# A prologue in another order on one Trainium2 core: scans, first normalisations, activation tables

## The reference

```python
x = x + attn(bi_wkv(x, f, f, w1, u1, cond))
x = x + ffn(bi_wkv(x, f, f, w2, u2, cond))
```

```python
def bi_wkv(r, k, v, w, u, cond):          # forward and backward scans over time
    tf = sigmoid(sum(cond)); decay = exp(-exp(w)) * (0.5 + 0.5 * tf)
    ek = exp(min(k, 30)); ekv = ek * v
    nf, df, nb, db = scans with a = a * decay + ekv, b = b * decay + ek
    euk = exp(min(u + k, 30))
    num = nf + nb - ekv + euk * v; den = df + db - ek + euk
    return sigmoid(r) * num / max(den, 1e-8) * (0.8 + 0.2 * tf)

def attn(x):                              # time mix, then channel mix
    h = layernorm(x) ; hp = h shifted by one step in time
    r, k, v = sigmoid(mix(h, hp) @ Wr), mix(h, hp) @ Wk, mix(h, hp) @ Wv
    x = x + (r * exp(u + k) * v / (exp(u + k) + 1e-8)) @ Wout
    h2 = layernorm(x)
    return x + sigmoid(mix(h2) @ cWr) * (square(relu(mix(h2) @ cWk)) @ cWv)

def ffn(x):                               # 32 experts, 8 for each token, and a shared one
    shared = square(relu(x @ up)) @ down
    routed = (sum over 8 experts of weight * square(relu(x @ fc1 @ w1[e])) @ w2[e]) @ fc2
    return shared + routed
```

## Time and profile before

| | |
|---|---|
| timed, median of 3 | 1136.41 us (1134.61 to 1138.21) |
| profiled execution | 1126.11 us |
| its span | 1124.4 us |
| TensorE products busy | 1048.5 us, 93% |
| TensorE weight loads busy | 649.4 us, 58% |
| VectorE busy | 724.5 us, 64% |
| ScalarE busy | 513.0 us, 46% |
| GpSimd busy | 472.0 us, 42% |

### The profile page before, as it was taken

How to read it: one execution, slowest core, us unless ns; L and a number is a source line. 1 busy time by engine, 2 the same in 40 slices (tenths; PEclk the granted TensorE clock), 3 DMA queues, 4 the chain that set the end, 5 groups by cost and what they waited for, 6 DMA issues and landing times.

```text
span 1124.4 us, 13091 instructions
## 1 busy us (share of the span) xinstructions
PE 1048.5 (93%) x4094; PEld 649.4 (58%) x4095; DVE 724.5 (64%) x1346; ACT 513.0 (46%) x778; POOL 472.0 (42%) x432
## 2 busy tenths in 40 slices
PE   0479999999999999999999999998999999999788
PEld 0344444444444444554644444446999999999788
DVE  8998449999999999870787000003555555555376
ACT  4465525656565556341221111113666666666211
POOL 3533003532353236220008777662666666666500
PEclk9999999999999999999999999999999999999889
DMA  4563024432643211321204685357766776677398
GB/s 149 173 213 101 1 38 138 151 101 59 204 151 101 64 39 33 101 38 75 75 1 139 216 286 191 143 174 205 161 157 157 157 156 157 157 157 157 115 405 299
DMA packets 186322, 157.23 MB, mean 140 GB/s; under 512 B 113824, under 2 KB 159392, under 8 KB 184224
## 3 DMA queue, kind: packets, MB, share of 16 engines
q1 hardware_dynamic: 170336, 113.12, 35.6%
q0 software_dynamic: 15936, 43.53, 12.3%
HBM read 67.09 MB, written 68.55 MB: 121 GB/s over the span
## 4 chain that ended last, share of the span: by engine, by line
PE 75%; DVE 17%; issue 4%; DMA 2%; ACT 1%; POOL 0%; ACTq 0%; POOLq 0%; SPq 0%; DVEq 0%
PE banks L1596 24%; PE banks L605 13%; PE banks L616 12%; PE banks L570 10%; PE banks L543 10%; PE banks L675 2%; PE banks L519 2%; DMA arena<-parts 2%; DVE arena L1345 2%; PE banks L1611 2%; DVE arena L1336 2%; DVE arena L1334 1%; DVE arena L1447 1%; DVE arena L1438 1%; PE banks L665 1%
## 5 line engine op out<-in xcount | busy, mean ns | idle before, releaser
L1596 PE MATMUL banks<-arena 128*128 128x512 f32 x896 | 389.7, 595 | 12.2 <-DVE arena L1399 5.1
L1596 PEld LDWEIGHTS banks<-arena 128*128 128x128 f32 x896 | 170.3, 191 | 228.7 <-issue 216.9
L482 POOL DMA_INDIRECT parts<-arena x160 | 171.0, 1069 | 126.4 <-DVE arena L879 101.3
L474 POOL DMA_INDIRECT slots_in<-arena x128 | 129.2, 1010 | 91.1 <-issue 87.1
L605 PEld LDWEIGHTS banks<-arena 128*128 128x128 f32 x1280 | 156.8, 194 | 7.9 <-issue 3.9
L605 PE MATMUL banks<-arena 128*128 128x128 f32 x1280 | 157.4, 277 | 3.0 <-ACT arena L713 3.0
L616 PE MATMUL banks<-arena 128*128 x640 | 151.1, 379 | 0.0
L879 DVE TENSOR_TENSOR arena<-banks,arena 128x512 f32<-128x512 f32 x80 | 55.3, 691 | 119.9 <-PE banks L616 119.9
L616 PEld LDWEIGHTS banks<-arena 128*128 128x128 f32 x640 | 115.6, 190 | 12.5
L543 PE MATMUL banks<-arena 128*128 128x512 f32 x256 | 114.3, 592 | 0.0
L570 PE MATMUL banks<-arena 128*128 128x512 f32 x256 | 114.1, 592 | 0.0
(11 more groups left out here) (179 smaller groups left out, 1239.7 us busy)
## 6 DMA issues: line engine op xcount, KB each, us to landing
slots_in<-arena SPq DMA_DIRECT2D x20, 1120.0 KB, 5.9
arena<-parts SPq DMA_DIRECT2D x16, 1024.0 KB, 10.0
arena<-fT SPq DMA_DIRECT2D x32, 256.0 KB, 2.8
arena<-w2T SPq DMA_DIRECT2D x4, 2048.0 KB, 13.6
arena<-xT SPq DMA_DIRECT2D x4, 1024.0 KB, 7.9
arena<-xT POOLq DMA_DIRECT2D x4, 1024.0 KB, 9.7
arena<-w1T SPq DMA_DIRECT2D x2, 2048.0 KB, 13.1
out<-arena SPq DMA_DIRECT2D x16, 256.0 KB, 6.9
```

Source lines behind the costliest of these rows:

```text
L474: pool.indirect_dma_start(rows_in, bass.IndirectOffsetOnAxis(ap=POSU[:, n, j:j + 1], axis=0), XLR[:, n].bitcast(mybir.dt.uint32), None).th ...
L482: pool.indirect_dma_start(parts, bass.IndirectOffsetOnAxis(ap=DESTU[:, g:g + 1], axis=0), YO[:, i % 4, c], None).then_inc(y_sent[i % 4], 16)
L1596: ins = pe.matmul(out, w[:, k, m * P:(m + 1) * P], x[:, k], start=(k == 0), stop=(k == kt - 1))
```

## The change

Nothing is computed otherwise, but the condition's sigmoid, which becomes 1 / (1 + exp(-s)), with the exponential on ScalarE and the rest on VectorE. Everything else is order, and the grain of waits:

- Start: ScalarE loads the logarithm and exponential set at once. VectorE makes only the first mix column, clips the first keys, and then makes the decays; the forward scans of item 0 run ahead of the tables that need ScalarE's logarithm; four mix columns follow behind. `pre` is split in `pre_keys` and `pre_bonus`.
- After the first items: forward scans and one backward scan of batch 1's tile 0 come ahead of y tiles 0 to 2; fin, y tile 3, clip, the other backward scan; centring and squares of batch 0 and 1 by tiles (`center_tiles`, `square_tiles`), the variance's products waiting for each; bonus; normalise, mixes. The slots of tiles 1, 2 and 3 follow the mixes.
- TensorE: rkv of batch 0 runs through, then batch 1's mean, and batch 1's variance lies inside the output product. Batch 1's first mix is handed over by tiles. On VectorE two residuals and the forward and first backward scan of iteration 1's first item stand ahead of batch 1's normalisation.
- Experts: the first `own_w1` no longer waits for the shared expert's last product; VectorE copies the first rows ahead of the last sum; TensorE's first `m1` waits for one sum less.

The core of the diff (declarations of semaphores and small waits are left out):

```diff
-            pe.wait_ge(S['down_evac'], K * B)
+            pe.wait_ge(S['down_evac'], K * B - 1)
             pe.wait_ge(S['w1_loaded'], 16 * 8)
             pe.wait_ge(S['w2_loaded'], 64)
             m1(0, 0, 0)
+            pe.wait_ge(S['down_evac'], K * B)
...
+            own_w1(0)
             act.wait_ge(S['down_mm'], K * B)
-            own_w1(0)
...
-            down(dve, 3)
+            for m in range(K - 1):
+                down_tile(dve, 3, m)
...
+            dve.wait_ge(S['down_mm'], K * B)
             xT(0)
+            down_tile(dve, B - 1, K - 1)
...
+            act.preload_act_table_set("natural_log_exp_and_others")
...
-            act.activation(tf, bank(7)[:, 0:B], ACT.Sigmoid).then_inc(S['cond_ready'], 1)
+            act.activation(tf, bank(7)[:, 0:B], ACT.Exp, scale=-1.0).then_inc(S['cond_ready'], 1)
...
+            def square_tiles(b):
+                dst = squares(1, b)
+                for k in range(K):
+                    act.wait_ge(*((S['z_tile'], (K - 1) * b + k + 1) if k < K - 1 else (S['z1_ready'], b + 1)))
+                    act.activation(dst[:, k], H[:, k], ACT.Square)\
+                       .then_inc(S['sq_tile'] if k < K - 1 else S['sq1_ready'], 1)
...
-            ln_exp()
+            pre_keys(first_items[0])
             act.wait_ge(S['rest_ready'], 1)
...
-            pre(first_items[0])
+            act.wait_ge(S['mix_columns'], len(MIXES))
+            act.wait_ge(S['shifts_ready'], 1)
+            pre_bonus(first_items[0])
...
-            slot(second_items[0], second_items[1])
-            square(1, 0)
-            pre(second_items[2])
+            pre(second_items[1])
+            square_tiles(0)
             rsqrt(1, 0)
-            post(second_items[1])
+            post(second_items[0])
             own(1, 0)
             gates(0, 0)
             ln_exp()
+            slot(second_items[1], second_items[2])
+            gates(0, 1)
+            sig_x(1)
+            ln_exp()
             slot(second_items[2], second_items[3])
-            sig_x(1)
-            gates(0, 1)
-            ln_exp()
-            post(second_items[3])
-            pre(body_items(1)[0])
             gates(0, 2)
             ln_exp()
-            square(1, 1)
+            pre(body_items(1)[0])
+            post(second_items[3])
+            gates(0, 3)
+            ln_exp()
+            square_tiles(1)
             rsqrt(1, 1)
-            gates(0, 3)
             own(1, 1)
...
+            def center_tiles(b):
+
+                dve.wait_ge(S['mean1_done'], b + 1)
+                for k in range(K):
+                    dve.tensor_tensor(H[:, k], xn(b, k), STAT, ALU.subtract)\
+                       .then_inc(S['z_tile'] if k < K - 1 else S['z1_ready'], 1)
...
+            dve.memset(eps_col, LN_EPS)
+            dve.memset(ones, 1.0).then_inc(S['ones_ready'], 1)
+            dve.memset(ZROW, 0.0).then_inc(S['zero_ready'], 1)
+            dve.wait_ge(S['params_loaded'], 32)
+            dve.wait_ge(S['ones_ready'], 1)
+            dve.tensor_scalar(tmu, vec[:, VECTORS.index('tm_u')], GATE_SHIFT, None, ALU.add)
+            for n in range(2):
+                ins = dve.tensor_copy(shift_b[:, n], vec[:, VECTORS.index(f'ln{n + 1}_b')])
+            ins.then_inc(S['shifts_ready'], 1)
+            mix_column(0)
+            clip(first_items[0])
+            dve.wait_ge(S['cond_ready'], 1)
+            step.did(dve.tensor_scalar(tf, tf, 1.0, None, ALU.add))
+            dve.memset(ones, 1.0 / C).then_inc(S['ones_ready'], 1)
+            step.wait()
+            step.did(dve.reciprocal(tf, tf))
+            step.wait()
+            step.did(dve.tensor_scalar(decay_b, tf, 0.5, 0.5, ALU.mult, ALU.add))
+            step.did(dve.tensor_scalar(out_scale, tf, -0.2, -0.8, ALU.mult, ALU.add))
+            step.wait()
+            for b in range(B):
+                step.did(dve.tensor_scalar(decay[:, :, :, b], wexp3, decay_b[:, b:b + 1], None, ALU.mult))
+            step.wait()
+
+            step.did(dve.tensor_copy(DECAY, decay))
+            step.did(dve.tensor_scalar(scratch32, decay, -1.0, 1.0, ALU.mult, ALU.add))
+            step.did(dve.tensor_scalar(rest, decay, 1.0, None, ALU.add))
+            step.wait()
+            step.did(dve.tensor_tensor(rest, rest, scratch32, ALU.mult))
+            step.wait()
+            dve.tensor_scalar(rest, rest, 1e-12, None, ALU.max).then_inc(S['rest_ready'], 1)
+            dve.wait_ge(S['rest_ready'], 1)
+            step.did(dve.reciprocal(scratch32, rest))
+            step.wait()
+            step.did(dve.tensor_tensor(over_rest, decay, scratch32, ALU.mult))
+            step.did(dve.tensor_scalar(floors, scratch32, DEN_FLOOR, None, ALU.mult))
+            step.did(dve.tensor_scalar(caps, scratch32, math.exp(KEY_CAP), None, ALU.mult))
+            step.wait()
+            fwd(first_items[0])
+            dve.wait_ge(S['log_exp'], 1)
+            step.did(dve.tensor_tensor(scratch32, bonus_b, rest, ALU.mult))
+            step.wait()
+            step.did(dve.scalar_tensor_tensor(log_rest, scratch32, -1.0, log_rest, ALU.add, ALU.add))
+            step.wait()
+            bonus = vec[:, 2:4].rearrange("p w (k o) -> p w k o", o=1).to_broadcast([P, 2, K, B])
+            dve.tensor_tensor(bonus_b, bonus, log_rest, ALU.subtract).then_inc(S['columns_ready'], 1)
+            for n in range(1, len(MIXES)):
+                mix_column(n)
+            dve.wait_ge(S['mix_columns'], len(MIXES))
             items = chain(second_items, body_items(1)[0])
             items[0]['prev'] = first_items[-1]
-            clip(first_items[0])
-            for it in first_items:
+            slot(first_items[0], begun=True)
+            for it in first_items[1:]:
                 slot(it)
+            it = items[0]
+            fwd(it)
+            dve.wait_ge(S['fwd_done'], it['i'] + 1)
+            back(it, 1).then_inc(S['bwd_done'], 1)
             y_stage(0, range(K - 1))
-            slot(items[0], lambda: y_stage(0, (K - 1,)))
-            center(1, 0)
-            slot(items[1])
+            fin(first_items[-1])
+            y_stage(0, (K - 1,))
+            clip(it['next'])
+            back(it, 0)
+            center_tiles(0)
+            bonus_den(it)
+            bonus_num(it)
             normalise(1, 0)
             mixes(1, 0)
+            slot(items[1])
+            product(0, 0)
             slot(items[2])
-            product(0, 0)
+            product(0, 1)
             slot(items[3])
-            product(0, 1)
+            product(0, 2)
+            y_stage(1, range(K - 1))
             fin(items[3])
-            y_stage(1)
-            product(0, 2)
-            center(1, 1)
-            normalise(1, 1, lambda: product(0, 3))
-            mixes(1, 1, between=lambda n: residuals(0, n))
+            y_stage(1, (K - 1,))
+            product(0, 3)
+            center_tiles(1)
+            residual(0, 0)
+            residual(0, 1)
+            ahead = body_items(1)[0]
+            fwd(ahead)
+            dve.wait_ge(S['fwd_done'], ahead['i'] + 1)
+            back(ahead, 1).then_inc(S['bwd_done'], 1)
+            normalise(1, 1, lambda: residual(0, 2))
+            mixes(1, 1, between=lambda n: residual(0, 3) if n == 0 else None)
...
+                    if tiles:
+                        pe.wait_ge(*((S['sq_tile'], (K - 1) * b + k + 1) if k < K - 1 else (S['sq1_ready'], b + 1)))
...
-            for m in range(3):
+            for m in range(K):
                 rkv(0, m)
             mean(1, 1)
-            rkv(0, 3, {1: lambda: var(1, 1)})
-            o_proj(0)
+            o_proj(0, {1: lambda: var(1, 1)})
```

More of the change, by code:

```diff
@@ L202, in by_tiles @@
         def by_tiles(which, b, n):
-            return which == 1 and b == 0 and n == 0
+            return which == 1 and b <= 1 and n == 0
         def squares(which, b):
@@ L1280, in _ @@
-            for n in range(2):
-                ins = dve.tensor_copy(shift_b[:, n], vec[:, VECTORS.index(f'ln{n + 1}_b')])
-            ins.then_inc(S['shifts_ready'], 1)
-            dve.wait_ge(S['mix_columns'], len(MIXES))
-            dve.wait_ge(S['cond_ready'], 1)
-            dve.memset(ones, 1.0 / C).then_inc(S['ones_ready'], 1)
-            step.did(dve.tensor_scalar(decay_b, tf, 0.5, 0.5, ALU.mult, ALU.add))
-            step.did(dve.tensor_scalar(out_scale, tf, -0.2, -0.8, ALU.mult, ALU.add))
@@ L1288, in _ @@
-            step.wait()
-            for b in range(B):
-                step.did(dve.tensor_scalar(decay[:, :, :, b], wexp3, decay_b[:, b:b + 1], None, ALU.mult))
-            step.wait()
-            step.did(dve.tensor_scalar(scratch32, decay, -1.0, 1.0, ALU.mult, ALU.add))
-            step.did(dve.tensor_scalar(rest, decay, 1.0, None, ALU.add))
-            step.wait()
-            step.did(dve.tensor_tensor(rest, rest, scratch32, ALU.mult))
-            dve.tensor_copy(DECAY, decay)
-            step.wait()
@@ L1307, in _ @@
-            step.wait()
```

(36 more changed lines are left out.)

50 lines of the change are left out of this document (17 added, 33 removed).

## The result

The changed kernel takes 1130.28 us (median of 16 runs, 1127.02 to 1135.75), the kernel before on the same chips 1137.85 (16 runs, 1133.85 to 1144.83). The ratio is 0.9941, 95% interval 0.9923 to 0.9959: 6.7 us faster, 4.7 to 8.8. The forecast was 11.0 us, to 1125.4. The sign and the mechanism of the prologue were right, the sum was 4.3 us too large.

A forecast was written before the change was run, and what follows sets the result against it. From its first product on, TensorE was taken to set the end, VectorE counting only where TensorE waits. 0 + 6.6 + 1.7 + 2.7 = 11.0 us off 1136.4 gave 1125.4; own range 1122.5 to 1128, wider range 1119.5 to 1130.5.

The forecast's parts named there:

- the prologue: Everything ahead of the experts: start 0, stretch to the first mix 6.6 us, moved slot hidden, batch 0 to batch 1 1.7.
- The profiled execution as a base: Gains read from the 1126.1 us profiled execution were taken off the 1136.4 median, 10.3 above, as no term depended on that.
- part 5: Experts' start: first weight copy no longer waits for the last shared product, TensorE starts at 773.0 instead of 774.04; gain 2.7 us.
- The clock term: Experts' start: idle of 1.3 instead of 2.30 us keeps the clock at 1.00; with it down all the same, gain 1.0.
- Part 1: Start to first backward scan: 0.76 us wait removed, 0.6 wait for keys and 0.4 dependent steps added; about 0, ends -0.5 and +0.5.
- Part 2: Fourth slot's end (42.52) to the first mix: reached at 66.7 instead of 73.27 us, 6.6 us earlier.
- The squares by tiles: Ahead of the first variance: they gain nothing, as warming products stand ahead of the variance in TensorE's queue, to 55.4 us.
- The collision: First normalisation: VectorE's multiplications fall on GpSimd's two for the fifth slot; cost taken as 1.9 us, ends 0 and 2.4.
- The clock was lost again: TensorE's first long products: the 1.9 us lost to the low clock before was left in, its absence kept as an end.
- Part 3: Slot moved behind the mixes, 7.9 us: hidden, with 2 to 3 us to spare before TensorE wants the last gating.
- Part 4: Batch 0 to batch 1: the 2.11 us gap goes, a 0.45 wait comes; gain 1.7 us.
- More: Rival: clock doesn't fall at the first product (1.9) and GpSimd misses the normalisation (1.9): 1121.6 us; chance 0.14.

The follow-up runs named there:

- f3: Changed kernel with GpSimd's first product behind the decays, ScalarE's fifth-slot pair ahead of the root, scatter's last four released by product 56 of 64: 1129.21 us, ratio 0.9905.
- e9: Changed kernel with GpSimd's scatter no longer held to TensorE's progress: 1230.94 us, ratio 1.0788 to the kernel before.
- f2: Same as f1, but with the experts' start as before the change: 1132.18 us, ratio 0.9945 to the kernel before.
- f4: Kernel before the change with only the scatter's hold loosened as in f1: 1138.61 us, ratio 1.0001 to the kernel before.
- f1: Changed kernel with GpSimd's first product behind the decays, ScalarE's fifth-slot pair ahead of the root, scatter's last four released by product 58, not 60: 1127.88 us, ratio 0.9926.
- e7: Changed kernel without the warming products ahead of the first variance, one profiled execution: batch 1's first product at 135.81 us, 2.4 later.
- e6: Changed kernel with ScalarE's fifth-slot logarithm and exponential ahead of the first reciprocal root, one profiled execution: root to first mix 4.51 us instead of 6.50.
- e5: Changed kernel with GpSimd's first product (the keys' values) held until the decays are done, one profiled execution: decays 0.63 us, first backward scan at 13.52.
- e10: Same as e9, but with the experts' start as before the change: 1238.43 us, ratio 1.0849 to the kernel before.

## Why the prediction was right and wrong

**The profiled execution as a base: this step failed.** "1136.4, lies 10.3 above that execution; no term depends on what makes that up" was wrong. Of the difference to a second trace of the same kernel, 9.03 us of 9.3 lie ahead of the experts, where stops hold up both TensorE and the scatter and the scatter ends last. One term depends on just that: part 5. The 2.30 us of idle, ended by ScalarE, were true of that execution; in the nine other traces with the same hold and loads it is 3.42 to 12.43 us, ended by the copy of the scattered rows. None of the rivals had the scatter in it.

**Part 5 (2.7): the term that failed.** About 0 instead: +0.7 us measured on the kernel before (-2.4 to +3.9), for the experts start 7.2 to 7.6 us behind the scatter's last instruction and not behind the last shared product. Where TensorE ends last the mechanics were right: 1.03 us of idle with the edit (f3, e9), against the 1.3 of the forecast. The clock term is the less certain half: with the free scatter 2.32 us of idle cost no clock (32 products in 3.81 us), and 2.33 in f2 did (5.44). Even 3.09 (f4) and 3.92 us (f1) cost none:

```profile
772.49 3.84 PE L605 MATMUL banks<-arena 128*128 128x128 f32 x32 [3.92 <-DVE arena L857]
```

**Part 1 (0):** +1.19. The waits were as forecast (0.73 for the keys against 0.6). What was missed is GpSimd's key product, now run while VectorE works on the decays: 1.07 us more for four small instructions, nearly all of it in one of them. The forecast listed what the moved steps change on VectorE and ScalarE, and not what they release on GpSimd.

**Part 2 (6.6):** right to 0.2 us for the stretch itself: 24.37 us (43.71 to 68.08) where 24.2 were put (42.52 to 66.7). The squares by tiles gained nothing, for the reason given, and e7 shows that taking the warming products away makes it worse. The collision, put at 1.9, measured 1.99 in e6. The clock was lost again (0.50 from 70 to 72 us). The Trainium skill's rule on the shared interfaces ("GPSIMD Engine Reference", Specifications) agreed once more in the gatings, 0.68 each alone and 1.72 each beside GpSimd; part 1's miss may be the same rule at a place where it was not looked for. The decays have one tensor in SBUF and a column of scalars; whether that falls under the rule's two inputs or its mode of two ports, no run shows.

**Part 3 (hidden):** right, but with 0.4 us to spare, as three gatings took 5.17 where 2.0 to 4.0 were put.

**Part 4 (1.7):** nearly right. The gap of 2.11 us went and one of 0.63 came, which is 1.5.

So the prologue was put at 8.3 and measured 6.7 in the trace (179.80 to 173.11) and 5.2 (2.2 to 8.2) by itself in time; the rest of the miss is part 5. **More** was a rival whose price was wrong: with the clock kept, 0.2 us came of 1.9, for the second mix was late by 1.25 anyway.

## What to carry to other kernels

Before a gap is priced, take a second trace of the same kernel, or at least explain why the profiled execution isn't at the median: what makes up that difference decides which wait ends last. A gain ahead of a steady stage arrives whole; one at a join of two chains counts only as far as the other chain is ahead, in the execution that usually comes. And when an operation is moved earlier, ask what it releases on GpSimd and what VectorE does in the next 1.3 us.

## What was not expected of the hardware

- Beside a GpSimd multiplication of 1.26 us one of four VectorE instructions on 128 x 8 elements took 1.29 us, the other three 0.22 or 0.23; all four took 1.70 together instead of 0.63. With the multiplication moved (e5), one of 128 x 32 took 0.97 instead of 0.19.
- 128 indirect scatters issued by GpSimd back to back (1.27 us each) left TensorE idle for up to 21 us at a time, and cost 90 us against before. Held back at every fourth, the scatter comes out of its waits up to 5 us late, four to seven times an execution, and at some of them other engines come out of theirs at the same moment. What passes between them, the traces don't show; that it isn't the weight loads is shown (scatter 185.95 us without them). How one execution of the fifteen traced with a hold escapes it stays open.
- An idle of 2.3 us ahead of TensorE's products cost clock in two traces (the first of before, 32 products in 5.44 us; f2, 5.44) and none in another (e10, 3.81); 3.09 us (f4, 3.81) and 3.92 (f1, 3.84) cost none, 3.80 (e6, 5.44) did. So the length of the idle alone doesn't tell.
- From the experts' first product on, four of eighteen traces were some 5 us longer than the others, and no trace says why.
